# Layer 0 of a two-layer megakernel: the softplus of dt is split differently over ScalarE, VectorE and GpSimd, and the normed x is transposed ahead of its block

## The chip, the cores and the metric

One core of a Trainium2 chip runs the whole program. The metric is device time in microseconds: the median of three runs of the kernel before is 2127.51 us (2127.39 to 2127.61). A core has a matrix engine (TensorE, PE in the rows), a vector engine (VectorE, DVE), an activation engine (ScalarE, ACT), GpSimd (POOL) and SyncE (SP), which here issues the transfers. Each engine works through its own instructions strictly in the order in which they are written; engines wait for one another by semaphores.

## The reference

Two layers over 32 sequences of 256 tokens of 128 features, each `x = x + attention(norm(x)) + ffn(norm(x))`. The change touches layer 0 alone, whose attention is a Mamba block and whose feed-forward is a dense mixture of eight experts:

```
xn = rmsnorm(layernorm(x));  xi, z = split(xn @ in_proj)
xi = silu(conv4(xi));  dt, B, C = split(xi @ x_proj)
delta = softplus(dt @ dt_w + dt_b)
h[t] = exp(delta*A) * h[t-1] + (delta*xi) * B;  y = sum_s h*C + xi*D
x + (y * silu(z)) @ out_proj
probs = softmax(layernorm(x) @ Wr + br); gate = probs kept up to a cumulated 0.8
ffn = sum_e gate_e * (relu(layernorm(x) @ W1_e + b1_e) @ W2_e + b2_e)
```

## The kernel before

Layer 0 cuts the 8192 tokens into 16 blocks of 512. A block has a **front** (norm, transposes, convolution, softplus, routing logits, gates, z) and a **body** of 32 slots. One body slot `h` is one tile of the scan (128 rows: 32 channels by 4 states, 512 tokens): ScalarE makes `dA = exp(delta*A)` (line 598), GpSimd makes `dBx` for two tiles at a time (733), VectorE scans (906) and multiplies by C (915) into `PR`, and TensorE sums the states (426). Beside it, one expert takes four slots: `UP` matmuls (405), relu into `hT` on ScalarE (607), `DN` matmuls (414), the gating into `GD` on ScalarE (614), the sum into `FF` on GpSimd (743).

All engines walk the same 32 slots, and in each slot they first do the slot's own work and then, in `fore`, those steps of the **next** block's front that a table places in this slot: `PE_AT`, `ACT_AT`, `DVE_AT`, `POOL_AT`, `SP_AT`, a slot number for each step. Slots -7 to -1 of a table are the last seven slots of the block before, for the front after the next. So the order of each engine is fixed by the numbers, and an engine that waits in one step holds back everything behind it in its order.

The steps that the change and the prediction speak of, by the names of the tables:

- TensorE: `dt0`, `dt1` (502) make the two halves of `dt @ dt_w` in the one PSUM bank `FRO`, so that `dt1` waits until ScalarE has read `dt0`; `xnt` (508) transposes the layernormed x, `logits` (514) multiplies it by `Wr`; `gt` (528) transposes the gates and waits for `z1`.
- ScalarE: `d0`, `d1` (643, 644) read the bank twice for each half, relu into `umax` and absolute value into `soft`; `exp` (684), `one` (688, 1+e), `ln` (692), `xn` (680, the copy of the transposed x); `gexp` (696), the exponential of the logits.
- VectorE: `soft` (981, (1+e)-1-e), `lnw` (991), `lg` (985), `z0` and `z1` (1001, 1011).
- GpSimd: `r` (799), `delta` (803), `lg` (806), `dx` (810), `rank` (820 to 830). Before each even slot's front steps it makes the `dBx` of the tiles two slots on, and it may do so only when the scan three tiles before these has ended, since `dBx` has two buffers.

softplus is computed as `max(u,0) + log1p(e)`, e = exp(-|u|), and log1p(e) as ln(1+e) where 1+e > 1, plus the small rest e - ((1+e)-1). In the buffers: `xch` holds `umax`, `soft` holds |u|, then e, then the rest, then delta; `tz` holds 1+e; `th` holds the logarithm.

Of the kernel before, what the change touches and what calls it, by code (L numbers as in the profile page):

```python
# [51 lines left out]
def layer0(nc, ctx, t, dram, scratch):  # L52
# [489 lines left out]
    def _(act):  # L542
# [169 lines left out]
    def _(pool):  # L712
# [1195 lines left out]
```

## Time and profile before

| | us |
|---|---|
| median of 3 runs | 2127.51 |
| profiled execution, first to last instruction (its span, the only time it has) | 2167.2 |
| layer 0 in it, to the last matmuls of its last block | about 1441 |
| busy: TensorE, weight loads | 1941.7, 1129.5 |
| busy: VectorE, ScalarE, GpSimd | 1681.5, 1340.8, 1310.3 |

The profiled execution is 1.9% longer than the median run; durations and sums below are on its scale. The page gives busy time per engine, a chain of waits and groups of instructions; the trace behind it gives each instruction's start, its duration, the idle time before it and what ended that idle time. Layer 0's steady part is 15 like periods, so one of them is read closely: that from 700 to 786 us.

### The profile page before, as it was taken

How to read it: one execution, taken by the hardware profiler on the slowest of the kernel's cores; microseconds unless marked ns; L12 is line 12 of the kernel's file. 1: busy time of each engine (PE TensorE's matmuls, PEld its weight loads, DVE VectorE, ACT ScalarE, POOL GpSimd, SP SyncE). 2: the span in 40 equal slices, each digit the busy share in tenths (PEclk: the TensorE clock that was granted, in tenths of full speed). 3: DMA queues.
4: the chain of work that ended last, by engine and by line, in shares of the span. 5: the costliest groups of instructions: out<-in, count | busy, mean ns of one | idle time of the engine just before them, and what ended most of it. 6: DMA issues, size and time to landing. Idle time of an engine off the chain costs nothing. (4 is left out here: it accounts for less than half of the span.)

```text
span 2167.2 us, 41765 instructions
## 1 busy us (share of the span) xinstructions
PE 1941.7 (90%) x14386; PEld 1129.5 (52%) x14386; DVE 1681.5 (78%) x2731; ACT 1340.8 (62%) x2423; POOL 1310.3 (60%) x1005
## 2 busy tenths in 40 slices
PE   5789999999999999999999999957999999988775
PEld 3455555555555555555555555534555555554442
DVE  5689888888798888887988888857888877774345
ACT  3677676776776777767767777631555555544343
POOL 2586886877867778778687787744433333325430
PEclk7999999999999999999999999976999999998787
DMA  8632633515425335154153362316444444454438
GB/s 205 145 93 56 137 81 80 136 36 124 105 47 134 84 75 138 39 120 112 43 137 84 70 136 66 82 45 174 120 115 123 116 114 116 118 155 129 119 95 239
DMA packets 212029, 235.27 MB, mean 109 GB/s; under 512 B 31590, under 2 KB 150414, under 8 KB 207694
## 3 DMA queue, kind: packets, MB, share of 16 engines
q1 hardware_dynamic: 207116, 227.98, 42.2%
q0 software_dynamic: 2048, 4.18, 0.7%
q8 instruction: 126, 2.06, 0.4%
q14 instruction: 99, 0.81, 0.1%
q10 hardware_dynamic: 2640, 0.24, 0.1%
HBM read 165.51 MB, written 66.85 MB: 107 GB/s over the span
## 5 line engine op out<-in xcount | busy, mean ns | idle before, releaser
L733 POOL TENSOR_TENSOR dBx<-REP,BC 128x1024 f32<-128x1024 f32 x256 | 604.2, 2362 | 260.1 <-DVE dA L906 227.7
L906 DVE TENSOR_TENSOR_SCAN dA<-dA,dBx 128x512 f32<-128x512 f32 x512 | 626.5, 1224 | 151.9 <-POOL dBx L733 105.8
L405 PE MATMUL UP<-xnT,W 128*128 128x512 f32 x1024 | 524.3, 631 | 56.7 <-ACT hT L607 43.4
L414 PEld LDWEIGHTS DN<-W,hT 128*128 128x128 f32 x4096 | 469.3, 192 | 99.4 <-issue 88.2
L414 PE MATMUL DN<-W,hT 128*128 128x128 f32 x4096 | 495.7, 278 | 0.3 <-ACT GD L614 0.3
L598 ACT ACTIVATE dA<-REP,A 128x512 f32<-128x512 f32 x512 | 354.2, 695 | 86.9 <-DVE PR L915 78.7
L607 ACT ACTIVATE hT<-UP,b 128x512 f32<-128x512 f32 x512 | 355.5, 694 | 78.6 <-PE UP L405 70.7
L915 DVE TENSOR_TENSOR PR<-dA,BC 128x512 f32<-128x512 f32 x512 | 353.6, 691 | 33.7 <-DVE dA L906 21.0
L405 PEld LDWEIGHTS UP<-xnT,W 128*128 128x128 f32 x1024 | 180.3, 195 | 296.6 <-issue 150.5
L1810 DVE TENSOR_REDUCE NM<-S 128x4 f32<-128x1024 f32 (+1 forms) x192 | 234.1, 1219 | 128.1 <-PE S L1355 76.8
L1569 ACT ACTIVATE PT<-S 128x1024 f32<-128x1024 f32 x192 | 197.1, 1026 | 124.5 <-PE S L1355 94.5
L614 ACT ACTIVATE GD<-DN,gate 128x128 f32<-128x128 f32 x512 | 145.8, 367 | 129.7 <-PE DN L414 128.5
L743 POOL TENSOR_TENSOR FF<-FF,GD 128x512 f32<-128x512 f32 x128 | 163.2, 1275 | 6.1 <-ACT GD L614 6.1
L426 PE MATMUL YS<-PR,fold 128*32 128x512 f32 x1024 | 141.8, 627 | 1.3 <-DVE y L921 0.7
L1623 POOL TENSOR_TENSOR t<-t 128x512 f32<-128x512 f32 x32 | 40.7, 1272 | 152.6 <-DVE t L1734 152.6
L1411 PE MATMUL OT<-PT,V 128*9 128x256 f32 x1024 | 87.7, 398 | 11.3 <-ACT PT L1569 7.9
L1550 ACT COPY CS<-ACC 128x256 f32<-128x256 f32 x64 | 23.8, 373 | 102.8 <-PE ACC L1467 102.8
L1629 POOL TENSOR_TENSOR SPL<-t,SPL 128x512 bf16<-128x512 f32 x32 | 37.1, 1160 | 79.3 <-ACT SPL L1575 79.3
L1563 ACT COPY OSB<-OT 128x512 f32<-128x512 f32 x64 | 37.5, 586 | 69.7 <-PE OT L1413 57.0
L426 PEld LDWEIGHTS YS<-PR,fold 128*32 128x32 f32 x1024 | 20.6, 110 | 106.8 <-issue 73.1
L972 DVE SCALAR_TENSOR_TENSOR xch<-FRO,convw,xch 128x510 f32<-128x510 f32 (+2 forms) x93 | 69.2, 744 | 8.6 <-ACT xch L657 6.4
L1376 PE MATMUL S<-KS,QS 50*128 50x256 bf16 x512 | 52.8, 285 | 13.4 <-DVE NM L1810 11.0
(251 smaller groups left out, 2667.1 us busy)
## 6 DMA issues: line engine op xcount, KB each, us to landing
BC<-s_b SPq DMA_DIRECT2D x128, 256.0 KB, 6.2
REP<-s_dx SPq DMA_DIRECT2D x124, 256.0 KB, 7.5
REP<-s_delta SPq DMA_DIRECT2D x124, 256.0 KB, 8.8
s_parts<-SPL SPq DMA_DIRECT2D x64, 192.0 KB
KS<-s_parts SPq DMA_DIRECT2D x64, 192.0 KB
QS<-s_parts SPq DMA_DIRECT2D x64, 192.0 KB
s_dx<-tz SPq DMA_DIRECT2D x16, 512.0 KB, 3.1
s_y<-zeros SPq DMA_DIRECT2D x32, 256.0 KB, 2.9
```

What stands on the lines that cost most here:

```text
L405: nc.tensor.matmul(UP[k % 2][:], W1[:, e % E0, f * P:(f + 1) * P], xnT[:, q, :], start=True, stop=True).then_inc(upf.sem, 1)
L414: last = nc.tensor.matmul(DN[:, j * P:(j + 1) * P], hT[:, e % 2, f, j * P:(j + 1) * P], W2[:, e, f, :], start=(f == 0), stop=(f == FB - 1))
L426: last = nc.tensor.matmul(YS[CB * j:CB * j + CB, :], fold[:], PR[:, (DB * b + j) % (2 * DB), :], start=(q == 0), stop=(q == NQ - 1), tile_ ...
L598: nc.scalar.activation(dA[:, k % 3, :], DR[:, h, j, :], ACT.Exp, scale=A[:, h, j, q:q + 1]).then_inc(da_ready.sem, 1)
L607: nc.scalar.activation(hT[:, e % 2, f, :], UP[k % 2][:], ACT.Relu, bias=b1[:, e % E0, f:f + 1]).then_inc(relu_done.sem, 1)
L614: last = nc.scalar.activation(GD[:, e % 2, j, :], DN[:, j * P:(j + 1) * P], ACT.Copy, scale=gate[:, par, j, e:e + 1])
L733: nc.gpsimd.tensor_tensor(dBx[:, s % 2], DX[:, h, j:j + 2, :], BC[:, q // 2, q % 2, :].unsqueeze(1).to_broadcast([P, 2, T0]), ALU.mult).th ...
L743: nc.gpsimd.tensor_tensor(FF[:, par], FF[:, par], GD[:, e % 2], ALU.add).then_inc(acc_done.sem, 1)
L906: nc.vector.tensor_tensor_scan(h, h, dBx[:, k // 2 % 2, k % 2, :], 0.0, ALU.mult, ALU.add).then_inc(scan_done.sem, 1)
L915: nc.vector.tensor_tensor(PR[:, k % (2 * DB), :], dA[:, k % 3, :], BC[:, q // 2, 2 + q % 2, :], ALU.mult).then_inc(prod_done.sem, 1)
L1569: nc.scalar.activation(PT[:, u // 3, u % 3, :], S2[:].rearrange("p b w -> p (b w)"), ACT.Exp, scale=SCALE).then_inc(exp_done.sem, 1)
L1810: nc.vector.tensor_reduce(NM[:, 0 if a == 0 else 1, :].rearrange("p (r i) -> p r i", r=2)[:, :, heads], S1[:].rearrange("p r (j k) -> p r ...
```

## The change

ScalarE reads each half of dt once (`u`, line 645 of the changed kernel) instead of twice, and `one` goes: `ln` takes 1+e by its own bias. VectorE now makes |u| by an AND on the bits and max(u, 0) (step `absu`, slot 15) and (1+e)-1 (step `wless`, slot 17, into `tz`) as three tensor-by-constant instructions over 128x1024; its old `soft` instruction goes, `lnw` stays. GpSimd has one more sum, `ue` = max + e in slot 17, and `r` subtracts `wless` from it in slot 19. `xnt` and its copy `xn` move from slots 17 and 18 to slot -1, right after the transpose `xqt` and its copy; `dt1` moves from slot 16 to 14, `d0` and `d1` from 14 and 16 to 13 and 14, `exp` from 17 to 16. Three waits for the transfers and buffers of the block before move from ScalarE to VectorE with the buffers that they guard.

```diff
-    PE_AT = dict(xqt=-2, x0=0, x1=4, out=8, xproj=10, dt0=12, dt1=16, xnt=17, logits=19, z0=23, z1=27, gt=29)
+    PE_AT = dict(xqt=-2, xnt=-1, x0=0, x1=4, out=8, xproj=10, dt0=12, dt1=14, logits=19, z0=23, z1=27, gt=29)
...
             if h == PE_AT["x0"]:
-                pe.wait_ge(xT_copied.sem, xT_copied.at(n, 1))
+                pe.wait_ge(xT_copied.sem, xT_copied.at(n, 2))
...
         def delta_input(k, n):
-            act.wait_ge(front.sem, front.at(n, 5 + k))
-            nc.scalar.activation(umax[:, k, :], bank(n, k)[:], ACT.Relu, bias=dtb[:, k:k + 1])
-            nc.scalar.activation(soft[:, k, :], bank(n, k)[:], ACT.Abs, bias=dtb[:, k:k + 1]).then_inc(u_done.sem, 1)
+            act.wait_ge(front.sem, front.at(n, 6 + k))
+            nc.scalar.activation(u[:, k, :], bank(n, k)[:], ACT.Identity, bias=dtb[:, k:k + 1]).then_inc(u_done.sem, 1)
...
             if h == ACT_AT["exp"]:
-                act.wait_ge(u_done.sem, u_done.at(n, 2))
+                act.wait_ge(log_step.sem, log_step.at(n, 1))
                 nc.scalar.activation(soft[:], soft[:], ACT.Exp, scale=-1.0).then_inc(sp_done.sem, 1)
-            if h == ACT_AT["one"]:
-                act.wait_ge(sp_done.sem, sp_done.at(n, 1))
-                act.wait_ge(e_stored.sem, e_stored.at(n - 1, 16))
-                nc.scalar.activation(one_w[:], soft[:], ACT.Identity, bias=1.0).then_inc(sp_done.sem, 1)
...
+                nc.scalar.activation(lnw[:], soft[:], ACT.Ln, bias=1.0).then_inc(sp_done.sem, 1)
...
+            if h == POOL_AT["ue"]:
+                pool.wait_ge(sp_done.sem, sp_done.at(n, 1))
+                pool.wait_ge(log_step.sem, log_step.at(n, 2))
+                nc.gpsimd.tensor_tensor(u[:], u[:], soft[:], ALU.add).then_inc(r_done.sem, 1)
             if h == POOL_AT["r"]:
-                pool.wait_ge(log_step.sem, log_step.at(n, 1))
-                nc.gpsimd.tensor_tensor(umax[:], umax[:], soft[:], ALU.subtract).then_inc(r_done.sem, 1)
+                pool.wait_ge(log_step.sem, log_step.at(n, 3))
+                pool.wait_ge(r_done.sem, r_done.at(n, 1))
+                nc.gpsimd.tensor_tensor(u[:], u[:], w_less[:], ALU.subtract).then_inc(r_done.sem, 1)
...
-            if h == DVE_AT["soft"]:
-                dve.wait_ge(sp_done.sem, sp_done.at(n, 2))
-                nc.vector.scalar_tensor_tensor(soft[:], one_w[:], -1.0, soft[:], ALU.add, ALU.subtract).then_inc(log_step.sem, 1)
+            if h == DVE_AT["absu"]:
+                dve.wait_ge(u_done.sem, u_done.at(n, 2))
+                dve.wait_ge(d_stored.sem, d_stored.at(n - 1, 16 * HALF))
+                dve.wait_ge(dx_done.sem, dx_done.at(n - 1, 1))
+                nc.vector.tensor_single_scalar(soft[:].bitcast(U32), u[:].bitcast(U32), SIGN - 1, ALU.bitwise_and).then_inc(log_step.sem, 1)
+                nc.vector.tensor_scalar(u[:], u[:], 0.0, None, ALU.max).then_inc(log_step.sem, 1)
+            if h == DVE_AT["wless"]:
+                dve.wait_ge(sp_done.sem, sp_done.at(n, 1))
+                dve.wait_ge(e_stored.sem, e_stored.at(n - 1, 16))
+                nc.vector.tensor_scalar(w_less[:], soft[:], 1.0, -1.0, ALU.add, ALU.add).then_inc(log_step.sem, 1)
```

TensorE, from the DN matmuls of slots 14 and 15 to the logits of slot 19; `FRO<-dtB,dtw` is dt1 and `FRO<-ident,XN` is xnt. Before:

```order
L414 MATMUL DN<-W,hT 128x128 x16
L405 MATMUL UP<-xnT,W 128x512 x2
L502 MATMUL FRO<-dtB,dtw 128x512
L405 MATMUL UP<-xnT,W 128x512 x2
L426 MATMUL YS<-PR,fold 32x512 x4
L508 MATMUL FRO<-ident,XN 128x128 x4
L414 MATMUL DN<-W,hT 128x128 x16
L514 MATMUL FRO<-Wr,xnT 128x8 x4
```

The same stretch of TensorE in the changed kernel:

```order
L416 MATMUL DN<-W,hT 128x128 x8
L504 MATMUL FRO<-dtB,dtw 128x512
L416 MATMUL DN<-W,hT 128x128 x8
L407 MATMUL UP<-xnT,W 128x512 x4
L428 MATMUL YS<-PR,fold 32x512 x4
L416 MATMUL DN<-W,hT 128x128 x16
L516 MATMUL FRO<-Wr,xnT 128x8 x4
```

dt1 now stands between the two halves of the DN matmuls, and xnt has left the stretch.

ScalarE, from the copy of the second half of dt (`xch<-FRO,dtb`) on, before; `soft<-soft` is exp, `tz<-soft` is one, `th<-tz` is ln:

```order
L643 ACTIVATE xch<-FRO,dtb 128x512
L644 ACTIVATE soft<-FRO,dtb 128x512
L607 ACTIVATE hT<-UP,b 128x512
L598 ACTIVATE dA<-REP,A 128x512
L607 ACTIVATE hT<-UP,b 128x512
L684 ACTIVATE soft<-soft 128x1024
L688 ACTIVATE tz<-soft 128x1024
L598 ACTIVATE dA<-REP,A 128x512
L680 COPY xnT<-FRO 128x512
L692 ACT_TABLE_LOAD
L692 ACTIVATE th<-tz 128x1024
L598 ACT_TABLE_LOAD
```

The same of ScalarE in the changed kernel:

```order
L645 ACTIVATE xch<-FRO,dtb 128x512
L600 ACTIVATE dA<-REP,A 128x512
L616 ACTIVATE GD<-DN,gate 128x128 x4
L609 ACTIVATE hT<-UP,b 128x512
L600 ACTIVATE dA<-REP,A 128x512
L609 ACTIVATE hT<-UP,b 128x512
L683 ACTIVATE soft<-soft 128x1024
L609 ACTIVATE hT<-UP,b 128x512
L600 ACTIVATE dA<-REP,A 128x512
L609 ACTIVATE hT<-UP,b 128x512
L600 ACTIVATE dA<-REP,A 128x512
L687 ACT_TABLE_LOAD
```

The copy of dt stands ahead of the gating GD, exp stands three instructions behind GD, and between exp and ln lie five instructions of the body.

GpSimd, around the softplus, before; `xch<-xch,soft` is r, `soft<-xch,th` is delta:

```order
L733 TENSOR_TENSOR dBx<-REP,BC 128x1024 x2
L743 TENSOR_TENSOR FF<-FF,GD 128x512
L733 TENSOR_TENSOR dBx<-REP,BC 128x1024
L799 TENSOR_TENSOR xch<-xch,soft 128x1024
L803 TENSOR_TENSOR soft<-xch,th 128x1024
L806 TENSOR_TENSOR lg<-lg,g 128x32
L733 TENSOR_TENSOR dBx<-REP,BC 128x1024
```

The same of GpSimd in the changed kernel, where `xch<-xch,soft` is the new ue and `xch<-xch,tz` is r:

```order
L728 TENSOR_TENSOR dBx<-REP,BC 128x1024
L795 TENSOR_TENSOR xch<-xch,soft 128x1024
L728 TENSOR_TENSOR dBx<-REP,BC 128x1024
L738 TENSOR_TENSOR FF<-FF,GD 128x512
L800 TENSOR_TENSOR xch<-xch,tz 128x1024
L728 TENSOR_TENSOR dBx<-REP,BC 128x1024
L804 TENSOR_TENSOR soft<-xch,th 128x1024
L807 TENSOR_TENSOR lg<-lg,g 128x32
L728 TENSOR_TENSOR dBx<-REP,BC 128x1024
```

ue stands ahead of the dBx of slot 18, so that this dBx, FF, r and the dBx of slot 20 now come after a wait for exp.

## Rows read from the trace of the kernel before

**Rows 1.** stretches: us, busy (instructions) PE PEld DVE ACT POOL, granted clock, DMA, GB/s
```profile
700.31:786.03 85.72, 82.58 (x446) 48.35 (x446) 72.93 (x90) 61.76 (x115) 65.71 (x44) 0.98 0.40 94
...
735.00:737.00 2.00, 2.00 (x3) 0.91 (x4) 2.00 (x4) 1.12 (x2) 2.00 (x3) 0.56 0.00 0
```

**Rows 2.** waits of PE, 100 to 1500 us: us in total, times, longest
```profile
PE UP L405 <- ACT hT L607: 42.5, 20, 2.6
...
PE FRO L528 <- DVE z L1011: 3.7, 10, 0.7
```

**Rows 3.** timeline of PE in one period: start us, us, what [idle before]
```profile
716.09 3.84 PE L414 MATMUL DN<-W,hT 128*128 128x128 f32 x32
...
721.57 1.12 PE L502 MATMUL FRO<-dtB,dtw 8*128 8x512 f32 x2
...
725.53 0.66 PE L508 MATMUL FRO<-ident,XN 128*128 128x128 f32 x4
...
734.99 3.58 PE L405 MATMUL UP<-xnT,W 128*128 128x512 f32 x4 [2.61 <-ACT hT L607]
...
759.06 0.27 PE L528 MATMUL FRO<-ident,gate 128*32 128x128 f32 x1 [0.30 <-DVE z L1011]
```

**Rows 4.** the same of ACT
```profile
719.96 1.14 ACT L614 ACTIVATE GD<-DN,gate 128x128 f32<-128x128 f32 x4 [1.40 <-PE DN L414]
...
722.73 0.72 ACT L643 ACTIVATE xch<-FRO,dtb 128x512 f32<-128x512 f32 x1
...
725.64 1.10 ACT L684 ACTIVATE soft<-soft 128x1024 f32<-128x1024 f32 x1
...
726.77 1.06 ACT L688 ACTIVATE tz<-soft 128x1024 f32<-128x1024 f32 x1
...
728.35 0.57 ACT L680 COPY xnT<-FRO 128x512 f32<-128x512 f32 x1
...
734.23 0.70 ACT L607 ACTIVATE hT<-UP,b 128x512 f32<-128x512 f32 x1
```

**Rows 5.** the same of POOL
```profile
716.95 2.38 POOL L733 TENSOR_TENSOR dBx<-REP,BC 128x1024 f32<-128x1024 f32 x1 [1.79 <-DVE dA L906]
...
726.53 2.37 POOL L733 TENSOR_TENSOR dBx<-REP,BC 128x1024 f32<-128x1024 f32 x1 [2.11 <-DVE dA L906]
...
730.06 2.35 POOL L799 TENSOR_TENSOR xch<-xch,soft 128x1024 f32<-128x1024 f32 x1 [1.16 <-DVE soft L981]
...
734.41 2.36 POOL L803 TENSOR_TENSOR soft<-xch,th 128x1024 f32<-128x1024 f32 x1 [2.00 <-DVE th L991]
...
736.93 2.35 POOL L733 TENSOR_TENSOR dBx<-REP,BC 128x1024 f32<-128x1024 f32 x1
...
739.24 1.27 POOL L743 TENSOR_TENSOR FF<-FF,GD 128x512 f32<-128x512 f32 x1
```

**Rows 6.** the same of DVE
```profile
727.86 2.12 DVE L981 SCALAR_TENSOR_TENSOR soft<-tz,soft 128x1024 f32<-128x1024 f32 x1 [0.68 <-ACT tz L688]
...
733.04 1.22 DVE L991 SCALAR_TENSOR_TENSOR th<-tz,th 128x1024 f32<-128x1024 f32 x1
...
749.96 1.23 DVE L906 TENSOR_TENSOR_SCAN dA<-dA,dBx 128x512 f32<-128x512 f32 x1 [4.10 <-POOL dBx L733]
...
758.24 0.68 DVE L1011 SCALAR_TENSOR_TENSOR z<-xch,FRO 128x512 f32<-128x512 f32 x1
```

**Rows 7.** one source line each: its instructions, min/median/max ns, first and last start
```profile
L981 DVE SCALAR_TENSOR_TENSOR soft<-tz,soft x16: 1225/2121/2886, 42.4 to 1326.8; 128x1024 f32<-128x1024 f32 x16
...
L886 DVE TENSOR_SCALAR outproj<-outproj x1: 275/275/275, 33.8 to 33.8; 128x256 f32<-128x256 f32 x1
...
L889 DVE TENSOR_SCALAR A<-A x1: 171/171/171, 34.1 to 34.1; 128x32 f32<-128x32 f32 x1
```

**Rows 8.** timeline of the start, DVE and POOL
```profile
12.85 1.01 DVE L897 TENSOR_SCALAR convb<-convb 128x2 f32<-128x2 f32 x1
...
12.76 1.07 POOL L782 TENSOR_TENSOR XN<-XI,mean 128x512 f32<-128x512 f32 x1 [10.56 <-DVE q L867]
```

More of the change, by code:

```diff
@@ L12 @@
 AX = mybir.AxisListType
+U32 = mybir.dt.uint32
 P = 128
@@ L38 @@
 FORGET, SLOWEST = 1e20, -1e-17
+SIGN = 1 << 31
 class Signal:
@@ L93, in layer0 @@
     xch = sb("xch", [P, HALF, T0]); th = sb("th", [P, HALF, T0]); tz = sb("tz", [P, HALF, T0]); soft = sb("soft", [P, HALF, T0])
-    umax, lnw, one_w, tanhz = xch, th, tz, xch
+    u, lnw, w_less, tanhz = xch, th, tz, xch
     delta, dx = soft, tz
@@ L202, in layer0 @@
     EARLY = 7
-    PE_AT = dict(xqt=-2, x0=0, x1=4, out=8, xproj=10, dt0=12, dt1=16, xnt=17, logits=19, z0=23, z1=27, gt=29)
-    ACT_AT = dict(xr=-2, tap0=2, tap1=4, tanh=6, dtb=10, d0=14, d1=16, xn=18, exp=17, one=17, ln=18, gexp=20, tz0=23, tz1=27, gt=29)
-    DVE_AT = dict(conv0=3, conv1=5, xi=8, soft=19, lg=19, lnw=20, gate1=23, z0=25, gate2=27, z1=29, ev1=3, store=9, stat=12, ev0=21)
-    POOL_AT = dict(xm=-7, xq=-4, xs=-4, ff=10, r=20, dx=23, rank=23, yz1=3, yz0=22, delta=20, lg=21, keep=27)
+    PE_AT = dict(xqt=-2, xnt=-1, x0=0, x1=4, out=8, xproj=10, dt0=12, dt1=14, logits=19, z0=23, z1=27, gt=29)
+    ACT_AT = dict(xr=-2, xn=-1, tap0=2, tap1=4, tanh=6, dtb=10, d0=13, d1=14, exp=16, ln=18, gexp=20, tz0=23, tz1=27, gt=29)
+    DVE_AT = dict(conv0=3, conv1=5, xi=8, absu=15, wless=17, lg=19, lnw=20, gate1=23, z0=25, gate2=27, z1=29, ev1=3, store=9, stat=12, ev0=21)
+    POOL_AT = dict(xm=-7, xq=-4, xs=-4, ff=10, ue=17, r=19, dx=23, rank=23, yz1=3, yz0=22, delta=20, lg=21, keep=27)
     GATE_AT = 3
@@ L510, in fore @@
             if h == PE_AT["logits"]:
-                pe.wait_ge(xT_copied.sem, xT_copied.at(n, 2))
+                pe.wait_ge(u_done.sem, u_done.at(n, 2))
                 for j in range(J0):
@@ L655, in fore @@
                         act.wait_ge(z_done.sem, z_done.at(n - 1, 2))
-                    act.wait_ge(front.sem, front.at(n, 2 + k))
+                    act.wait_ge(front.sem, front.at(n, 3 + k))
                     nc.scalar.activation(xch[:, k, :], bank(n, k)[:], ACT.Identity, scale=convw[:, k, 3:4], bias=convb[:, k:k + 1]).then_inc(tap_done.sem, 1)
@@ L663, in fore @@
             if h == ACT_AT["dtb"]:
-                act.wait_ge(front.sem, front.at(n, 4))
+                act.wait_ge(front.sem, front.at(n, 5))
                 act.wait_ge(b_stored.sem, b_stored.at(n - 1, 16))
@@ L678, in fore @@
                 act.wait_ge(upf.sem, upf.at(n - 2, E0 * FB))
-                act.wait_ge(front.sem, front.at(n, 7))
+                act.wait_ge(front.sem, front.at(n, 2))
                 nc.scalar.copy(xnT[:, q, :], FRO[:]).then_inc(xT_copied.sem, 1)
             if h == ACT_AT["exp"]:
-                act.wait_ge(u_done.sem, u_done.at(n, 2))
+                act.wait_ge(log_step.sem, log_step.at(n, 1))
                 nc.scalar.activation(soft[:], soft[:], ACT.Exp, scale=-1.0).then_inc(sp_done.sem, 1)
-            if h == ACT_AT["one"]:
+            if h == ACT_AT["ln"]:
                 act.wait_ge(sp_done.sem, sp_done.at(n, 1))
-                act.wait_ge(e_stored.sem, e_stored.at(n - 1, 16))
-                nc.scalar.activation(one_w[:], soft[:], ACT.Identity, bias=1.0).then_inc(sp_done.sem, 1)
-            if h == ACT_AT["ln"]:
-                act.wait_ge(sp_done.sem, sp_done.at(n, 2))
-                nc.scalar.activation(lnw[:], one_w[:], ACT.Ln).then_inc(sp_done.sem, 1)
+                nc.scalar.activation(lnw[:], soft[:], ACT.Ln, bias=1.0).then_inc(sp_done.sem, 1)
             if h == ACT_AT["gexp"]:
@@ L776, in fore @@
                     pool.wait_ge(stat_step2, 21)
-                pool.wait_ge(front.sem, front.at(n - 1, 7))
+                pool.wait_ge(front.sem, front.at(n - 1, 2))
                 pool.wait_ge(xi_loaded.sem, xi_loaded.at(n, 16))
@@ L988, in fore @@
             if h == DVE_AT["lnw"]:
-                dve.wait_ge(sp_done.sem, sp_done.at(n, 3))
-                nc.vector.scalar_tensor_tensor(lnw[:], one_w[:], 1.0, lnw[:], ALU.is_gt, ALU.mult).then_inc(log_step.sem, 1)
+                dve.wait_ge(sp_done.sem, sp_done.at(n, 2))
+                dve.wait_ge(log_step.sem, log_step.at(n, 3))
+                nc.vector.scalar_tensor_tensor(lnw[:], w_less[:], 0.0, lnw[:], ALU.is_gt, ALU.mult).then_inc(log_step.sem, 1)
             if h == DVE_AT["gate1"]:
```

17 lines of the change are left out of this document (7 added, 10 removed).

## Prediction, made before the result was known

> **What bounds the kernel now.** I read the stretches first: in one steady period of 85.72 us TensorE is busy 82.58, VectorE 72.93, GpSimd 65.71, ScalarE 61.76 [rows 1]. So TensorE sets the pace, and what it loses is worth looking for. Its list of waits names one large entry, 42.5 us for ScalarE's relu (`hT`), and a small one that matters more than its size, 3.7 us for VectorE's `z1` [rows 2]. The timelines of one period show both.
>
> The large one is a pile on ScalarE. exp, one, a dA, the copy of the transposed x, a table load, ln and a second table load follow one another from 725.64 on, and the relu that TensorE needs starts only at 734.23 [rows 4]. TensorE stands 2.61 us before 734.99 [rows 3]; after that stand its granted clock reads 0.56 for 735 to 737, so for most of that time it is at the lower of its two levels, 1.2 instead of 2.4 GHz, and over the whole period the reading is 0.98: 2% of 85.72, or 1.7 us of work, lost [rows 1]. Stall and slow clock together are 2.61 + 1.7 = 4.3 us of a period.
>
> The small one says that a second path is as late as TensorE in spite of that stall. GpSimd begins delta at 734.41 and from there has no gap: lg, dBx at 736.93, FF [rows 5], y, dx, the rank steps and one more dBx. VectorE's scan at 749.96 had waited 4.10 us for that last dBx, its z1 follows at 758.24 [rows 6], and TensorE's `gt` at 759.06 had waited 0.30 us for z1 [rows 3]. So between the softplus and gt the period hangs on GpSimd's order about as much as on the pile: in 10 periods gt waits for z1 [rows 2].
>
> **The change on ScalarE and TensorE.** Of the pile go `one` (1.06), the copy of x (0.57) and two of the four reads of dt (0.72 each) [rows 4]; exp moves ahead by a slot. This empties some 2.7 us between the relus of slots 17 and 20, so most of the 2.61 us stall goes. But dt1 now stands between the two halves of DN. These began at 716.09 and took 3.84 [rows 3], so dt1 starts near 718.0 and ends 1.12 later [rows 3], at 719.1; ScalarE's second copy of dt, 0.72 [rows 4], ends at 719.8. The second half of DN ends at 721.0 instead of 719.9, and ScalarE's gating GD, which waits for it, starts there instead of at 719.96 [rows 4]. exp now stands behind GD, a relu, a dA and a relu; the same four took 722.73 - 719.96 = 2.77 before [rows 4]. So exp starts at 723.8 and, at 1.10 [rows 4], ends at 724.9: 1.9 earlier than now, not a whole pile earlier.
>
> **On VectorE.** The three new instructions read one buffer in SBUF and write another, 1024 columns. The rows have 275 ns for 256 columns and 171 for 32 [rows 7], 0.46 ns a column, so 0.63 us each as an estimate; the bounds are 0.28 (no dearer than 256 columns) and 1.22 (the 1024 columns of lnw [rows 6]). Added 1.9, removed 2.12 of the old `soft` instruction [rows 6]: even. absu holds the scans of slots 16 and later from about 717.6 to 719.8, until dt is read; VectorE waited several times in that stretch for dA, so I cost this at nothing up to lg, which waits for the logits in any case. lnw stands behind lg and a scan, so it comes hardly earlier than its 733.04 [rows 6]: by 0.66 at most, the time of xnt, which no longer stands ahead of the logits [rows 3].
>
> **On GpSimd.** Here the change adds 2.36 (delta's duration for the same shape [rows 5]) and, above all, a wait in a strict order. GpSimd ends slot 16's dBx at 716.95 + 2.38 = 719.3 [rows 5] and then stands at ue until exp ends, 724.9: 5.6 us in which slot 18's dBx waits too, though its own condition is met. From 724.9 it does, without a gap, ue 2.36, dBx 2.37, FF 1.27, r 2.35, dBx 2.37, and delta and lg in the 2.52 between 734.41 and 736.93 [rows 5]. That is 13.2, so the next dBx starts at 738.1 instead of 736.93: **+1.2**.
>
> To this comes the SBUF path that VectorE and GpSimd cannot use at once. The old `soft` took 1.23 when GpSimd stood and up to 2.89 otherwise [rows 7]; in this period it started at 727.86 while a dBx ran from 726.53 to 728.90 [rows 5], and took 2.12, which is the rest of that dBx and 1.1 more. A tensor-by-constant instruction suffers likewise: one over two columns, at 12.85, took 1.01 us, to the end of the GpSimd instruction that ran from 12.76 for 1.07 [rows 8]. Now lnw becomes ready near 733, in the middle of GpSimd's gapless row, and delta needs it: whichever goes first, 1.1 is put into the row: **+1.1**. wless and ue both wait for exp: if VectorE is first, ue starts 0.6 later, if GpSimd is first, VectorE waits 2.36 and GpSimd nothing: 0 to 0.6, I take **+0.2**, nearer to the row in which GpSimd held the path. The Trainium skill, SBUF — State Buffer, section Who interferes with whom, says that a VectorE instruction on a tensor and a constant can take the pair of ports shared with GpSimd and that whoever issues first holds it for the whole instruction. Here the trace agrees (1.01 us for two columns); without this rule the +0.2 would be zero, and a reader who counted the instructions alone would miss it and the +1.1.
>
> From that dBx to gt nothing is shortened: the same GpSimd row, the scan that already waits for it, z1, gt. So gt shifts by 2.5, and TensorE, which comes there earlier by the stall it was spared, waits there, or just ahead at the relu of slot 28.
>
> **From gt to the next dt1** TensorE is the pace, and xnt now stands there: **+0.6** of its 0.66 [rows 3]. Its copy on ScalarE, 0.57 [rows 4], lies in slot -1 beside the UP matmuls of slot 0; x0 waits for it, with the UPs of slot 1 queued behind. If that cover failed it would cost 0 to 0.6; I take nothing. The waits moved to VectorE are for steps of the block before, 24 slots back: nothing.
>
> Sum: 1.2 + 1.1 + 0.2 + 0.6 = 3.1 us a period. Of the 16 blocks (42.4 to 1326.8 between the first and last `soft`, 85.6 apart [rows 7]) 15 have their front beside a body; the first of these is irregular, I count 14: 43 us. In block 0's front xnt and its copy stand ahead of x0, 1.2 us once, and two reads of dt and `one` go: nothing. The profiled span is 2167.2 against the median of 2127.51, a ratio of 0.98: 43 becomes 42.5, so **2170 us**.
>
> **Rivals.**
> - *The pile was all that mattered* (faster). TensorE gains up to 4.3 a period: 15 x 4.3 x 0.98 = 63, so 2064, or, partly, to 2115. For it: 42.5 us of waits, the largest entry [rows 2], and 20 us of a period in which GpSimd is idle [rows 1]. Against: gt already waits for z1, and delta cannot start earlier than lnw allows. It needs exp to end some 3 us ahead of my 724.9, or z1 not to bind. Chance 0.12.
> - *GpSimd's row is no later than now* (no change): the 5.6 us stand is absorbed because delta waits for lnw anyway. Then gt moves by -0.7 to 0 and xnt adds 0.6: 2126 to 2136. For it: GpSimd's waits of 1.16 and 2.00 before r and delta [rows 5], which ue could fill. Against: the sum of the row, which is longer than these. Chance 0.10.
> - *The shared path costs nothing* (less slow): +1.2 + 0.6 = 1.8 a period, 25 us: 2152. Chance 0.08.
> - *TensorE's clock falls at the new stand* (slower still). Its wait ahead of gt would be about as long as the 2.61 after which it fell [rows 1, 3]; if it falls there, the loss of up to 1.7 is paid where TensorE is the pace: 4.4 to 4.8 a period, 2189 to 2193. It decides wherever the stand before slot 28's relu exceeds that of now; if the clock falls at an earlier stand, the next one hides it. Chance 0.13.
>
> **Numbers.** The forecast has 0.57, its own range 2155 to 2182. About 0.2% (4 us) is what a measurement of this kernel tells from no change. Faster: the first rival and a little of the second, 0.14; the same 0.07; slower 0.79. The range 2122 to 2192 leaves out most of the first rival and the end of the last.
>
> **What would show it.** In the changed kernel: GpSimd idle about 5.6 us before ue, ended by exp; VectorE idle about 2 us before absu, ended by the copy of dt; TensorE's 2.61 stand before the relu of slot 20 down to 1 or less, and in its place waits ahead of gt or at slot 28's relu; lnw or wless stretched beyond 1.3 and 0.7; the dBx behind lg 2 to 3 us later. From the start of slot 14's DN matmuls to the dBx behind lg it is 736.93 - 716.09 = 20.8 us now and 23.3 by my sum. I am wrong if that distance stays at 21 or less, or if gt does not wait for z1.

## The result, and the profile after

The changed kernel takes 2176.79 us (median of 4 runs, 2175.67 to 2179.83) against 2127.45 for the kernel before, run beside it: a ratio of 1.0238, 95% interval 1.0224 to 1.0253. It is slower by 49.3 us. The forecast was 2170, in a range from 2122 to 2192. Below, a *stand* is time in which an engine waits idle, the *pile* is ScalarE's run of instructions from exp to the second table load, the *row* is GpSimd's run of instructions from the end of exp to delta, and the *shared path* is the way to SBUF on which VectorE and GpSimd hold each other up (the old `soft` took 1.23 us, or 2.12 beside a dBx [rows 6, 7]).

The loss lies in layer 0. Its last output matmuls, in the timeline of TensorE before and in the changed kernel (start us, us, what):

```profile
1437.52 3.78 PE L438 MATMUL FRO<-outproj,y 128*128 128x128 f32 x16
```

```profile
1485.33 3.78 PE L440 MATMUL FRO<-outproj,y 128*128 128x128 f32 x16
```

Layer 0 ends 47.8 us later.

Two distances describe where a period grew, both taken in the trace for 12 of the 14 regular periods and averaged: from the start of the matmul dt0 to the start of GpSimd's delta, and from delta to TensorE's `gt`. The first went from 22.26 to 25.17 us. The second is 24.67 before and 24.69 after. Everything behind delta (lg, dBx, dx, the rank steps, a dBx, a scan, z1) takes its fixed time, and `gt` follows. The rest of the period, from `gt` to the next dt0, went from 39.15 to 39.58. The sum of these changes is 3.4 us a period. From the dt0 at 193.57 before (194.26 after) 13 regular periods lose 44.1 us, the irregular one ahead of them 0.5, and the last front with the body behind it 3.0: with 0.2 at the start, the 47.8.

GpSimd in the changed kernel, in two neighbouring periods, to be set beside [rows 5] (start us, us, what [idle before <- what ended it]; line 795 is ue, 800 r, 804 delta):

```profile
654.97 2.36 POOL L795 TENSOR_TENSOR xch<-xch,soft 128x1024 f32<-128x1024 f32 x1 [5.84 <-ACT soft L683]
...
663.59 2.36 POOL L728 TENSOR_TENSOR dBx<-REP,BC 128x1024 f32<-128x1024 f32 x1
667.19 2.35 POOL L804 TENSOR_TENSOR soft<-xch,th 128x1024 f32<-128x1024 f32 x1 [1.24 <-DVE th L1001]
...
669.69 2.36 POOL L728 TENSOR_TENSOR dBx<-REP,BC 128x1024 f32<-128x1024 f32 x1
...
737.64 2.35 POOL L728 TENSOR_TENSOR dBx<-REP,BC 128x1024 f32<-128x1024 f32 x1 [2.06 <-DVE dA L907]
745.91 2.91 POOL L795 TENSOR_TENSOR xch<-xch,soft 128x1024 f32<-128x1024 f32 x1 [5.92 <-ACT soft L683]
748.76 2.38 POOL L728 TENSOR_TENSOR dBx<-REP,BC 128x1024 f32<-128x1024 f32 x1
...
752.30 2.38 POOL L800 TENSOR_TENSOR xch<-xch,tz 128x1024 f32<-128x1024 f32 x1
754.61 3.36 POOL L728 TENSOR_TENSOR dBx<-REP,BC 128x1024 f32<-128x1024 f32 x1
757.93 2.36 POOL L804 TENSOR_TENSOR soft<-xch,th 128x1024 f32<-128x1024 f32 x1
...
760.44 2.36 POOL L728 TENSOR_TENSOR dBx<-REP,BC 128x1024 f32<-128x1024 f32 x1
```

These lines show the stand of 5.8 to 5.9 us before ue, ended by exp, and behind it, in the second period, a row without a gap up to the dBx behind lg. VectorE in the same two periods, beside [rows 6] (984 is absu, 990 wless, 1001 lnw, 1021 z1):

```profile
655.04 2.85 DVE L990 TENSOR_SCALAR tz<-soft 128x1024 f32<-128x1024 f32 x1
...
663.96 3.07 DVE L1001 SCALAR_TENSOR_TENSOR th<-tz,th 128x1024 f32<-128x1024 f32 x1
...
740.81 0.69 DVE L984 TENSOR_SCALAR soft<-xch 128x1024 uint32<-128x1024 uint32 x1 [2.53 <-ACT xch L645]
...
745.91 0.68 DVE L990 TENSOR_SCALAR tz<-soft 128x1024 f32<-128x1024 f32 x1
...
754.02 1.74 DVE L1001 SCALAR_TENSOR_TENSOR th<-tz,th 128x1024 f32<-128x1024 f32 x1
...
781.72 0.68 DVE L1021 SCALAR_TENSOR_TENSOR z<-xch,FRO 128x512 f32<-128x512 f32 x1
```

The regular periods come in two kinds, in turn; only the last two are alike. In the one at 745, VectorE's wless gets the shared path first (0.68) and ue is 0.55 longer; later lnw makes a dBx 1.0 longer. In the one at 655, ue is first, wless takes 2.85, lnw 3.07, and delta waits 1.24 us for lnw. Both kinds begin delta at the same distance from dt0 (at 641.96 and 732.81), 25.2 and 25.1 us.

TensorE's waits from 100 to 1500 us, beside [rows 2] (us in total, times, longest), and its timeline in these periods, beside [rows 3]:

```profile
PE UP L407 <- ACT hT L609: 45.5, 34, 3.0
PE YS L428 <- DVE y L922: 29.7, 15, 3.3
...
PE FRO L530 <- DVE z L1021: 9.0, 11, 0.9
```

```profile
668.95 1.94 PE L428 MATMUL YS<-PR,fold 128*32 128x512 f32 x8 [3.33 <-DVE y L922]
670.81 5.43 PE L416 MATMUL DN<-W,hT 128*128 128x128 f32 x32
...
691.81 0.27 PE L530 MATMUL FRO<-ident,gate 128*32 128x128 f32 x1 [0.18 <-DVE z L1021]
...
736.77 2.05 PE L416 MATMUL DN<-W,hT 128*128 128x128 f32 x16
...
754.16 2.31 PE L407 MATMUL UP<-xnT,W 128*128 128x512 f32 x4 [0.80 <-ACT hT L609]
...
778.31 2.81 PE L407 MATMUL UP<-xnT,W 128*128 128x512 f32 x4 [2.77 <-ACT hT L609]
781.05 1.93 PE L428 MATMUL YS<-PR,fold 128*32 128x512 f32 x8
782.91 0.40 PE L530 MATMUL FRO<-ident,gate 128*32 128x128 f32 x1
```

The stand of 2.61 us [rows 3] is down to 0.80, as the change wants. TensorE waits more than before all the same, at other places: before YS in slot 21, for VectorE's y, which stands behind lnw; at the relu of slot 28; and at `gt` for z1. The granted clock (third number from the end) falls behind the two longest stands of these lines, 3.33 and 2.77 us; 0.50 is the lower of its two levels, and 0.61 over 8 us is the lower one for most of them:

```profile
668.00:676.00 8.00, 7.05 (x40) 5.42 (x41) 7.70 (x12) 3.19 (x6) 8.00 (x6) 0.61 0.19 65
...
781.00:783.00 2.00, 2.00 (x10) 0.29 (x10) 1.97 (x4) 0.69 (x1) 1.96 (x2) 0.50 1.09 238
```

### The profile page after: what moved, and what is told of

Same layout as the page of the kernel before. It is cut to its first block and busy times, and to the rows that moved or that the text cites. A ratio compares the mean times of both kernels' runs of the same rounds, so it can differ in the third digit from the quotient of the medians.

```text
span 2175.0 us, 41789 instructions
## 1 busy us (share of the span) xinstructions
PE 1937.9 (89%) x14386; PEld 1130.6 (52%) x14386; DVE 1706.2 (78%) x2763; ACT 1299.9 (60%) x2375; POOL 1359.0 (62%) x1021
## 5 line engine op out<-in xcount | busy, mean ns | idle before, releaser
L728 POOL TENSOR_TENSOR dBx<-REP,BC 128x1024 f32<-128x1024 f32 x256 | 613.7, 2399 | 207.4 <-DVE dA L907 181.2
L416 PEld LDWEIGHTS DN<-W,hT 128*128 128x128 f32 x4096 | 477.2, 194 | 122.6 <-issue 111.1
L416 PE MATMUL DN<-W,hT 128*128 128x128 f32 x4096 | 507.6, 281 | 0.3 <-ACT GD L616 0.3
L428 PE MATMUL YS<-PR,fold 128*32 128x512 f32 x1024 | 141.9, 627 | 30.3 <-DVE y L922 29.7
L795 POOL TENSOR_TENSOR xch<-xch,soft 128x1024 f32<-128x1024 f32 x16 | 42.1, 2632 | 108.4 <-ACT soft L683 108.4
```

The costliest lines, as they stand in the source:

```text
L416: last = nc.tensor.matmul(DN[:, j * P:(j + 1) * P], hT[:, e % 2, f, j * P:(j + 1) * P], W2[:, e, f, :], start=(f == 0), stop=(f == FB - 1))
L428: last = nc.tensor.matmul(YS[CB * j:CB * j + CB, :], fold[:], PR[:, (DB * b + j) % (2 * DB), :], start=(q == 0), stop=(q == NQ - 1), tile_ ...
L728: nc.gpsimd.tensor_tensor(dBx[:, s % 2], DX[:, h, j:j + 2, :], BC[:, q // 2, q % 2, :].unsqueeze(1).to_broadcast([P, 2, T0]), ALU.mult).th ...
```

## The experiments

The theory to test: the loss is the row of GpSimd from exp to delta (the added sum, which waits for exp and stands in order ahead of a dBx) and what lnw and wless put into it on the path shared with VectorE; the moved transposes cost little. Rivals: the moved transposes, the place of dt1 between the halves of DN, absu's wait, the collisions alone. All runs are in one table. Times are medians; ratios are to the kernel before on the same chip, with 95% intervals; the columns on the right are us, averaged as above, in the one run of each kernel that was profiled. e3 does not compute the softplus, e7 and e8 leave out its correction of the rounding, e6, e9, e10 and e11 lnw's mask. In the edits shown, `.then_inc(...)` at the end of a line and some of the waits are left out, and `...` marks a cut.

| run | us | ratio | exp ends after dt0 | dt0 to delta | delta to gt | gt to dt0 |
|---|---|---|---|---|---|---|
| before | 2127.45 | 1 | 14.62 | 22.26 | 24.67 | 39.15 |
| changed | 2176.79 | 1.0238 (1.0224-1.0253) | 12.93 | 25.17 | 24.69 | 39.58 |
| e1_xnt_alone | 2129.87 | 1.0017 (1.0005-1.0028) | 14.62 | 21.87 | 24.66 | 39.82 |
| e2_early_alone | 2147.02 | 1.0103 (1.0089-1.0118) | 12.94 | 23.68 | 24.69 | 38.81 |
| e3_sum_unbound | 2141.59 | 1.0079 (1.0064-1.0094) | 12.94 | 22.84 | 24.67 | 39.46 |
| e4_sum_on_vector | 2163.66 | 1.0172 (1.0157-1.0187) | 12.94 | 24.45 | 24.70 | 39.58 |
| e5_absu_later | 2178.24 | 1.0249 (1.0227-1.0272) | 12.93 | 25.15 | 24.73 | 39.44 |
| e6_no_mask | 2162.92 | 1.0171 (1.0149-1.0194) | 12.93 | 24.11 | 24.91 | 40.02 |
| e7_no_correction | 2097.59 | 0.9869 (0.9846-0.9893) | 12.93 | 18.54 | 26.09 | 39.62 |
| e8_before_no_correction | 2116.50 | 0.9955 (0.9927-0.9982) | 14.60 | 19.24 | 26.87 | 39.25 |
| e9_sum_behind_dbx | 2157.52 | 1.0164 (1.0141-1.0186) | 12.94 | 23.63 | 24.83 | 39.62 |
| e10_candidate | 2109.41 | 0.9925 (0.9905-0.9944) | 14.61 | 21.09 | 24.65 | 39.07 |
| e11_candidate_xnt | 2114.93 | 0.9946 (0.9926-0.9965) | 14.61 | 21.09 | 24.64 | 39.47 |

**e1: the moved transposes alone, on the kernel before.**

```diff
-PE_AT: xnt=17    ACT_AT: xn=18
+PE_AT: xnt=-1    ACT_AT: xn=-1
```

> The kernel before, with nothing changed but the transposes of the normed x and their copy (xnt, xn), which move to slot -1. Theory (GpSimd's order with the added sum is the loss, the moved transposes cost at most their own 0.66 us where TensorE is the pace): at most 15 x 0.6 = 9 us slower, and as the copy of 0.57 leaves the pile on ScalarE some of it comes back: 2120 to 2137. Rival (the moved transposes and the order of x0 behind them carry the loss): 2160 to 2177.

Measured 1.0017: 3.7 us. Between `gt` and dt0 0.67 us a period are lost, and 0.39 come back between dt0 and delta. The rival falls.

**e2: the early places alone.** The kernel before with dt1, d0, d1, exp and one in the changed kernel's slots.

```diff
-PE_AT: dt1=16    ACT_AT: d0=14, d1=16, exp=17, one=17
+PE_AT: dt1=14    ACT_AT: d0=13, d1=14, exp=16, one=16
```

> The kernel before, softplus as it was (two reads of dt and one on ScalarE, soft on VectorE, no added sum on GpSimd), but at the changed kernel's stand: dt1 in slot 14, d0 in 13, d1 in 14, exp and one in 16. Theory (GpSimd's added sum and its stand are the loss, not the stand of dt1 between the halves of DN): the pile in slots 17 to 19 is broken up and nothing is added to GpSimd: 2095 to 2130. Rival (dt1 between the halves of DN, and what waits for dt, is the loss): 2150 to 2177.

Measured 2147.02, between the two ranges: 21 us slower with nothing added on GpSimd, so the theory's part on the early places falls. ScalarE, then VectorE in this run, whose dt0 starts at 716.25:

```profile
725.33 1.14 ACT L614 ACTIVATE GD<-DN,gate 128x128 f32<-128x128 f32 x4
```

```profile
731.47 1.23 DVE L906 TENSOR_TENSOR_SCAN dA<-dA,dBx 128x512 f32<-128x512 f32 x1 [1.75 <-ACT dA L598]
...
733.34 2.88 DVE L981 SCALAR_TENSOR_TENSOR soft<-tz,soft 128x1024 f32<-128x1024 f32 x1
...
738.57 1.21 DVE L991 SCALAR_TENSOR_TENSOR th<-tz,th 128x1024 f32<-128x1024 f32 x1
```

exp ends 1.68 us earlier, but delta starts 1.42 later. Two things hold VectorE's scans. With dt1 between the halves of DN, ScalarE's GD, which waits for the second half, starts 9.08 us behind dt0 instead of 7.84 (719.96 [rows 4], behind the dt0 at 712.12); the next dA and its scan come about as much later. Then exp and one stand ahead of one more dA, and its scan waits 1.75 us for it. soft follows that scan and takes 2.88 us instead of 2.12 [rows 6], as it collides with a dBx. An earlier exp is worth nothing here as long as the scans that stand ahead of lnw on VectorE come later. How much of the 21 us is dt1's place, the rival, and how much exp's, no run tells.

**e3: the sum without its wait.**

```diff
-                pool.wait_ge(sp_done.sem, sp_done.at(n, 1))
...
-                nc.gpsimd.tensor_tensor(u[:], u[:], soft[:], ALU.add)
+                nc.gpsimd.tensor_tensor(u[:], u[:], u[:], ALU.add)
...
-                nc.gpsimd.tensor_tensor(u[:], u[:], w_less[:], ALU.subtract)
+                nc.gpsimd.tensor_tensor(u[:], u[:], w_less[:], ALU.add)
```

> The changed kernel with GpSimd's added sum in its place and of the same size, but adding max to itself, so that it does not wait for exp; the next sum adds where it subtracted, which keeps the values finite. The softplus is left out so far: delta is not the reference's. Theory (GpSimd's stand until exp and the gapless row after it): the sum runs in what was the stand of 5.9 us, the row after exp is 2.4 us shorter, terms 1.2 and 0.2 of the 3.1 a period go, and part of the 1.1: 2136 to 2150. Rival 1 (the work of 2.36 us on GpSimd, wherever it runs): 2170 to 2180. Rival 2 (the shared SBUF path alone: lnw and wless collide with other GpSimd work as before): 2165 to 2177.

Measured 1.0079: the ratio falls by 0.0159, 34 of the 49 us, as the theory expected. GpSimd in this run:

```profile
726.36 1.89 POOL L794 TENSOR_TENSOR xch<-xch 128x1024 f32<-128x1024 f32 x1 [2.20 <-DVE xch L984]
...
735.85 2.35 POOL L728 TENSOR_TENSOR dBx<-REP,BC 128x1024 f32<-128x1024 f32 x1
739.89 2.36 POOL L803 TENSOR_TENSOR soft<-xch,th 128x1024 f32<-128x1024 f32 x1 [1.69 <-DVE th L1000]
```

The sum runs in what was the stand, the row has room again and delta waits for VectorE's lnw, as before. The sum of one buffer with itself is 0.47 cheaper than that of two; as GpSimd waits 1.27 us behind it, this changes nothing. Some of the loss stays, 0.58 us a period up to delta and 0.31 from `gt` to dt0: with the row out of the way delta waits for lnw, which ends 22.8 us behind dt0 instead of 22.1.

**e4: the sum on VectorE.**

```diff
-                nc.gpsimd.tensor_tensor(u[:], u[:], soft[:], ALU.add)
...
-                nc.vector.tensor_scalar(u[:], u[:], 0.0, None, ALU.max)
...
+                nc.vector.scalar_tensor_tensor(u[:], u[:], 0.0, soft[:], ALU.max, ALU.add)
```

> The changed kernel with the added sum on VectorE instead of GpSimd: one instruction, max(u, 0) + e, takes the place of max and of GpSimd's sum. Theory: GpSimd's row from exp on is 2.4 us shorter and it stands for nothing, the relief at TensorE's stand of 2.61 us stays and xnt still costs 0.6 a period: 2100 to 2130, from the start of slot 14's DN matmuls to the dBx behind lg 21 us or less. Rival 1 (collisions on the shared SBUF path, with one more VectorE instruction to collide): 2165 to 2180. Rival 2 (xnt or the stand of dt1): 2165 to 2177.

Measured 2163.66: the theory's range ends 34 us below, and the rivals' begins 1.3 above. VectorE, then GpSimd:

```profile
744.07 1.79 DVE L983 TENSOR_SCALAR tz<-soft 128x1024 f32<-128x1024 f32 x1 [0.48 <-ACT soft L683]
745.79 2.29 DVE L984 SCALAR_TENSOR_TENSOR xch<-xch,soft 128x1024 f32<-128x1024 f32 x1
```

```profile
742.94 2.37 POOL L728 TENSOR_TENSOR dBx<-REP,BC 128x1024 f32<-128x1024 f32 x1 [4.75 <-DVE dA L901]
...
748.15 2.36 POOL L794 TENSOR_TENSOR xch<-xch,tz 128x1024 f32<-128x1024 f32 x1 [1.16 <-DVE xch L984]
...
755.52 2.35 POOL L798 TENSOR_TENSOR soft<-xch,th 128x1024 f32<-128x1024 f32 x1 [2.02 <-DVE th L995]
```

Now GpSimd waits for VectorE. The two instructions run into slot 18's dBx and the FF behind it and take 4.08 us, where wless and lnw without a collision take 0.68 and 1.20 (the shortest of each in the changed kernel): some 2.2 more. Three scans follow before lnw. So the theory is too narrow: between exp and delta the two engines make one chain, and a sum taken off one is paid, here for the most part, on the other. That is rival 1 in kind, the collisions of one more VectorE instruction.

**e5: absu a slot later.**

```diff
-DVE_AT: absu=15
+DVE_AT: absu=16
```

> The changed kernel with absu and max one slot later on VectorE (16 for 15), so that one more scan and product run while VectorE would stand 2.5 us for the copy of dt. Theory 1 (only GpSimd's row from exp on counts): no change, 2172 to 2180, as exp has 2.5 us of slack behind absu. Theory 2 (VectorE's own row from dt0 to lnw, its waits included, is the pace in the periods in which GpSimd takes the shared path first): 0.5 to 1.9 us off such a period or off each: 2150 to 2170.

Measured 1.0249, no change: theory 1 holds and theory 2 falls. VectorE's wait for dt shrinks from 2.53 to 0.50 us, and a wait for exp takes its place; absu's wait costs nothing:

```profile
739.81 0.69 DVE L984 TENSOR_SCALAR soft<-xch 128x1024 uint32<-128x1024 uint32 x1 [0.50 <-ACT xch L645]
...
744.87 0.69 DVE L990 TENSOR_SCALAR tz<-soft 128x1024 f32<-128x1024 f32 x1 [1.90 <-ACT soft L683]
```

**e6: without lnw.**

```diff
-                pool.wait_ge(log_step.sem, log_step.at(n, 4))
+                pool.wait_ge(sp_done.sem, sp_done.at(n, 2))
...
-                nc.vector.scalar_tensor_tensor(lnw[:], w_less[:], 0.0, lnw[:], ALU.is_gt, ALU.mult)
```

> The changed kernel without lnw, the instruction on VectorE that sets the logarithm to zero where 1 + e rounds to 1; delta takes ScalarE's logarithm as it is (this part of the softplus is left out). Theory 1 (GpSimd's row; lnw puts 1.1 us into it by the shared path): 1.1 off a period, 2157 to 2163. Theory 2 (VectorE's row): in one kind of period lnw takes 3.07 us and ends the row, in the other 1.74: 1.1 to 2.5 off a period, 2140 to 2160. If collisions do not matter: 2170 to 2177.

Measured 1.0171: 0.0067, or 14 us. Delta starts 1.06 earlier; theory 1 had 1.1, and its range ends at 2163. GpSimd's row is now of the kind without a gap in every regular period: delta at 752.67 follows straight on the dBx from 750.36 for 2.37. Not all of it reaches the end of the period: from delta to `gt` 0.22 is lost again, from `gt` to dt0 0.44, and in the trace layer 0 ends 9.9 us earlier (1479.2 against 1489.1). The other 4 us of the 14 are not in layer 0 of that trace.

**e7 and e8: without the correction of the rounding, on the changed kernel and on the one before.**

```diff
-                nc.gpsimd.tensor_tensor(u[:], u[:], soft[:], ALU.add)
-                nc.gpsimd.tensor_tensor(u[:], u[:], w_less[:], ALU.subtract)
-                nc.vector.tensor_scalar(w_less[:], soft[:], 1.0, -1.0, ALU.add, ALU.add)
-                nc.vector.scalar_tensor_tensor(lnw[:], w_less[:], 0.0, lnw[:], ALU.is_gt, ALU.mult)
...
-                nc.gpsimd.tensor_tensor(umax[:], umax[:], soft[:], ALU.subtract)
-                nc.vector.scalar_tensor_tensor(soft[:], one_w[:], -1.0, soft[:], ALU.add, ALU.subtract)
-                nc.vector.scalar_tensor_tensor(lnw[:], one_w[:], 1.0, lnw[:], ALU.is_gt, ALU.mult)
```

> The changed kernel without the correction of the rounding: GpSimd's sums ue and r and VectorE's wless and lnw are left out, delta is max(u, 0) + ln(1 + e). Both theories: neither GpSimd nor VectorE holds gt any more, TensorE goes from dt0 to gt in some 44.7 us instead of 49.9 (17.8 to the logits, 11.5 to z0, 9.6 to z1, 5.9 to gt, the shortest of the runs so far) and pays 0.65 for the moved transposes: 1.5 to 1.9 a period under before, 2098 to 2108. Rival (the stand of dt1 between the halves of DN, the moved transposes and absu's wait cost by themselves): 2127 or more.

> The kernel before without the same correction: soft and lnw on VectorE and r on GpSimd are left out, the rest stands where it stood. Theory (before is held at about the same length by TensorE with ScalarE's pile and by the other two engines): the pile of slots 17 to 19 and TensorE's stand of 2.61 us remain, gt loses only its wait of 0.3: 2118 to 2128. Rival (VectorE and GpSimd alone set the pace of before, the pile costs nothing): 2095 to 2110.

The first four lines are e7's, the last three e8's. Measured 0.9869 and 0.9955, 2097.59 and 2116.50 us: 0.4 and 1.5 under the theory's ranges, and both rivals' ranges are missed; e8's single runs lie 31 us apart (2098.87 to 2129.99). With delta that early its distance to `gt` grows (26.09, 26.87). In e8 TensorE sets the pace, `gt` waits for nothing, and only now does the pile count. e8 has the old stand and, in this period, a slow clock behind it (3.61 for 2.31 us of UP), e7 still has 0.81 us before the relu of slot 20. In e7 `gt` waits for z1 after all, 15 times: the dBx behind lg waits 1.38 us for a scan that stands behind the logits on VectorE, and from that dBx to `gt` it is 22.1 us, as before (759.06 - 736.93 [rows 3, 5]). TensorE, then GpSimd in e7, then TensorE in e8:

```profile
719.28 2.31 PE L407 MATMUL UP<-xnT,W 128*128 128x512 f32 x4 [0.81 <-ACT hT L609]
...
742.58 0.27 PE L530 MATMUL FRO<-ident,gate 128*32 128x128 f32 x1 [0.84 <-DVE z L1001]
```

```profile
720.43 2.37 POOL L728 TENSOR_TENSOR dBx<-REP,BC 128x1024 f32<-128x1024 f32 x1 [1.38 <-DVE dA L897]
```

```profile
725.51 3.61 PE L405 MATMUL UP<-xnT,W 128*128 128x512 f32 x4 [2.60 <-ACT hT L607]
```

Without the correction the change gains 2116.50 - 2097.59 = 19 us. That is what removing the pile and all else in the change bring together, and it comes only where nothing else holds delta; as e7 is held by z1, it does not say what TensorE alone could win.

**e9: e6 with the sum behind slot 18's dBx.**

```diff
-POOL_AT: ue=17
+POOL_AT: ue=18
```

> The kernel of the run without the mask (lnw left out), in which GpSimd's row from exp on has no gap in any period, with one thing more: GpSimd's added sum stands in slot 18, behind that slot's dBx and FF, in place of ahead of them. Theory (the row is gapless from exp on, and dBx of slot 18 was ready at 11.9 us behind dt0 where exp ends at 13.0): the row starts 1.1 us earlier, 2163 - 15 x 1.1 = 2147. Rival (slot 18's dBx could not start before exp's end anyway, as VectorE's scan 17 is late): 2158 to 2166.

Measured 2157.52, just outside the rival's range and 10 us from the theory's number. Its ratio to the kernel before is 1.0164, that of e6 1.0171, so the times do not tell the two apart; in the traces delta comes 0.48 earlier, of the 1.1 us. VectorE's order is why: its scan 17 (there from 736.99) ends at 738.2, 12.5 us behind dt0, and only then can the dBx start.

```profile
738.29 2.37 POOL L728 TENSOR_TENSOR dBx<-REP,BC 128x1024 f32<-128x1024 f32 x1 [5.36 <-DVE dA L907]
```

**e10 and e11: a candidate, without and with the moved transposes.** e10 is the kernel before without `one` and lnw:

```diff
-                nc.scalar.activation(one_w[:], soft[:], ACT.Identity, bias=1.0)
...
-                nc.scalar.activation(lnw[:], one_w[:], ACT.Ln)
+                nc.scalar.activation(lnw[:], soft[:], ACT.Ln, bias=1.0)
...
-                nc.vector.scalar_tensor_tensor(soft[:], one_w[:], -1.0, soft[:], ALU.add, ALU.subtract)
+                nc.vector.tensor_scalar(one_w[:], soft[:], 1.0, -1.0, ALU.add, ALU.add)
+                nc.vector.tensor_tensor(one_w[:], one_w[:], soft[:], ALU.subtract)
...
-                nc.vector.scalar_tensor_tensor(lnw[:], one_w[:], 1.0, lnw[:], ALU.is_gt, ALU.mult)
```

> A candidate, the kernel before with less in it: no one on ScalarE (the logarithm adds the 1 itself, as in the changed kernel), no mask lnw; VectorE makes (1 + e) - 1 in 0.69 us and subtracts e in one more instruction, so GpSimd keeps its two sums. Theory (before hangs on TensorE with the pile and on the row of the other two engines about equally; both get shorter): the pile loses 1.06 of TensorE's stand of 2.61 us and with it some of the 1.7 us of slow clock, delta begins about 2 us earlier as lnw no longer holds it: 1 to 2.7 us a period, 2085 to 2112. Rival (VectorE's two instructions are held up on the shared path by slot 18's dBx, r and delta come no earlier): 2118 to 2130.

> The same candidate with the transposes of the normed x and their copy moved to slot -1 as in the changed kernel. Theory: the pile loses 0.57 more and the logits come 0.4 earlier, the transposes cost 0.65 to 0.88 ahead of x0: within 6 us of the candidate on either side, 2085 to 2115. Rival (with the pile nearly gone, what is left of the stand and of the slow clock goes too): 10 us or more under the candidate.

e10 takes 2109.41, 0.9925 of the kernel before, within the range expected: it is faster than both, by 16 us (under 1%, with the whole interval below 1) and by 67. Delta starts 1.17 earlier, 15 x 1.17 = 17.6 us. GpSimd, then VectorE in e10:

```profile
723.94 2.36 POOL L795 TENSOR_TENSOR xch<-xch,tz 128x1024 f32<-128x1024 f32 x1 [1.89 <-DVE tz L980]
726.38 2.35 POOL L799 TENSOR_TENSOR soft<-xch,th 128x1024 f32<-128x1024 f32 x1
```

```profile
720.25 2.35 DVE L978 TENSOR_SCALAR tz<-soft 128x1024 f32<-128x1024 f32 x1
```

delta follows on r without the 2.00 us that it waited for lnw [rows 5]. The rival's collision is there as well: the first of VectorE's two instructions takes 2.35 us for 0.69, and r starts 18.7 us behind dt0, 17.9 before, which is why 1.17 came and not 2. In e11 delta is where it is in e10, and 0.40 us a period are lost between `gt` and dt0. The medians lie 5.5 us apart, within what was expected; the two ratios' intervals overlap, so it is the trace more than the time that speaks for leaving the transposes of the normed x where they were.

## Why the prediction was right, and where not

The signs that the prediction named came: the stand before ue, VectorE's stand of 2.53 us before absu, 0.80 for 2.61 us before the relu of slot 20, lnw and wless stretched, the dBx behind lg later, and `gt` waiting for z1, 11 times.

- *exp ends 1.9 earlier, not a whole pile.* It ends 1.69 earlier (14.62 and 12.93).
- *GpSimd stands 5.6 us at ue, the row behind it is gapless.* 5.92 and 5.84; from exp's end (12.93 behind dt0 at 732.81) to the dBx at 760.44 it is 14.7 us, by the prediction 13.2 + 1.1 + 0.2 = 14.5. From slot 14's DN matmuls to that dBx 760.44 - 736.77 = 23.7, foretold 23.3.
- *lnw puts 1.1 into the row.* Taking lnw out brought delta 1.06 earlier (e6). The rows show the collisions: 3.36 us for a dBx of 2.37, 2.85 for a wless of 0.68. The Trainium skill, SBUF — State Buffer, section Who interferes with whom, says that whoever issues first has the shared ports for the whole instruction and that the other blocks. The trace agrees: that wless ends at 657.89, 0.56 behind the ue that started ahead of it. That the two take turns from period to period was not foreseen: the terms of 1.1 and 0.2 hold in one kind of period only, while in the other VectorE is the later one, by 1.24 us. Both kinds cost the same, and that this made the sum come out right is luck.
- *VectorE is even, and absu's wait costs nothing up to lg.* Of absu this holds (e5). But that the new places hold VectorE's scans was not seen: e2 loses 21 us by them without any sum on GpSimd. In the changed kernel VectorE's order comes out about as late as the row, in one kind of period later, while the sum had the row alone.
- *xnt costs 0.6.* Between `gt` and dt0 it is 0.43 in the changed kernel and 0.67 in e1. That delta comes 0.39 earlier in e1 the sum had at nothing; there it pays for more than half, in the changed kernel the row eats it.
- *The moved waits cost nothing.* In the changed kernel VectorE's idle time ahead of absu is ended by the copy of dt all 15 times, and ahead of wless there is none.
- *The sum, 3.1 us a period.* Measured are 3.4: 2.9 for 2.5 up to delta, 0.4 for 0.6 from `gt` on. For 14 periods the difference is 3.6 us. Shrinking 43.4 to 42.5 by the ratio of median to profiled span took 0.9. But 2167.2 - 1441.3 = 725.9 us of that execution lay behind layer 0, against 2175.0 - 1489.1 = 685.9 after, and 682 to 690 in the profiles of the experiments, in a layer that the change doesn't touch: the slack of the profile was elsewhere, and durations of layer 0 needed no scale. The last 2.3 of the 6.8 us between 2170 and 2176.8 lie outside the 14 periods, 0.8 of them in layer 0; where the other 1.5 lie, the profiles do not tell.
- *TensorE sets the pace* was the weakest step. The distance from delta to `gt` is the same within 0.3 us in all runs but e7 and e8, and before the change `gt` came 46.9 us behind dt0 in twelve periods running. So already then delta decided when `gt` came, and TensorE's stand of 2.61 us with its slow clock was slack. But the slack was small, as the prediction had it with its second path as late as TensorE: in e8, with the same pile and nothing else in the way, `gt` comes 45.2 to 46.9 us behind dt0. The 42.5 us of waits [rows 2] looked like the largest entry to win; breaking up the pile while delta is held longer wins nothing (e2), and 19 us came where the correction was gone (e7 against e8). The small entry, 3.7 us for z1, was the bound. The first rival falls with this, and so do the one with no change and the one without collisions (e6).
- *The clock falls at the new stand* came true in the period at 745 at the relu of slot 28 (0.50 from 781 to 783), at a price of half a us: `gt` ran at 782.91, and z1 had ended at 781.72 + 0.68 = 782.40. Only four of the 14 periods pay it (25.0 to 25.1 from delta to `gt`, 24.5 to 24.7 in the others). In the period at 655 it falls behind YS, at a wait that I had not seen at all (29.7 us in 15 times), and the delay is over before `gt`, which waits 0.18 for z1.

What stays open: why the turn between wless and ue alternates from one period to the next, what the transposes' 0.43 to 0.67 us depend on, and what dt1's place between the halves of DN costs by itself.

## What to carry to other kernels

When several in-order engines share a period, take the distances between a few events (a start, the step that several engines need, the next step of the busiest engine) in the profile before. One that is the same in every period is a candidate for the pace, as delta to `gt` was here, and the busiest engine's largest wait may be slack. Here a short wait of that engine at the end of the chain said more than a long one in its middle. Between two engines that share a path and feed each other, count one chain: here a sum moved from one to the other brought back 14 of 49 us, and an input made earlier cost 21 with the places that were moved for it, while less work in the chain was a gain on either kernel (14 and 16 us).

## What the runs showed of the hardware

- Two instructions on VectorE and GpSimd that one event releases do not always go in the same order: at wless and ue the order alternated between neighbouring periods (0.68 with 2.91, 2.85 with 2.36).
- The time that an instruction is held on the shared path is shown as its own busy time, not as idle: lnw took from 1.20 to 3.07 us.
- An AND on 32-bit words took VectorE as long as max on as many floats, and as wless where nothing held it: 0.69 us for 1024 columns, all 16 between 0.685 and 0.698.
- GpSimd's sum of a buffer with itself took 1.89 us, that of two buffers 2.36, both over 1024 columns.
